# Token rows of attention move from the maxima's PSUM ring to the scores' ring, with a copy on ScalarE and the division on GpSimd

## What is computed

```python
xn = _layernorm(x, axis=-1)
x = x + _L0_attn_ref(xn, Wq, Wk, Wv) + _L0_ffn_ref(xn, w_gate, w_in, w_out)
```

## Time and profile before

| | |
|---|---|
| runs shown | 1012.16, 1012.63, 1015.68 us; median 1012.63 |
| the profiled execution | 1011.26 us, its span (first to last instruction) 1009.1 us |
| granted TensorE clock, mean of the span | 0.995 of full |
| busy share of the span | PE 98%, PEld 51%, DVE 79%, ACT 68%, POOL 17% |
| TensorE in the chain that ended last | 95% |
| attention loop, 380 to 980 us, in each 100 us | DVE 93 to 97 us, ACT 87 us, POOL 7 to 8 us |

### The profile page before, as it was taken

One profiled execution on the slowest core, in us unless ns is written; L12 is line 12 of the kernel. 1 busy time (PEld: TensorE's weight loads), 2 busy tenths in 40 slices (PEclk: granted clock), 3 DMA queues, 4 the chain that ended last, 5 costly groups with the idle time before them and its releaser, 6 DMA issues.

```text
span 1009.1 us, 20754 instructions
## 1 busy us (share of the span) xinstructions
PE 984.5 (98%) x7816; PEld 515.8 (51%) x7816; DVE 800.7 (79%) x1023; ACT 682.0 (68%) x1355; POOL 175.7 (17%) x325
## 2 busy tenths in 40 slices
PE   7999999999998999999999999999999999999995
PEld 6888888888876333333333333333333333333332
DVE  4343455543466899999999999999999999999967
ACT  2212333333322788888888888888888888888884
POOL 2001445444455100000000000000000000000000
PEclk9999999999999999999999999999999999999997
DMA  9967442223300233333333333333334333332204
GB/s 354 369 238 219 138 146 69 74 70 106 101 9 1 59 91 92 94 85 96 89 96 91 91 94 86 100 87 96 89 92 94 86 96 89 97 90 70 73 18 167
DMA packets 127043, 108.59 MB, mean 108 GB/s; under 512 B 81120, under 2 KB 102368, under 8 KB 126944
## 3 DMA queue, kind: packets, MB, share of 16 engines
q1 hardware_dynamic: 122720, 102.81, 35.3%
q10 hardware_dynamic: 4224, 4.46, 1.3%
HBM read 80.75 MB, written 42.21 MB: 122 GB/s over the span
## 4 chain that ended last, share of the span: by engine, by line
PE 95%; DVE 2%; issue 1%; DMA 1%; POOL 1%; SPq 0%; ACT 0%; POOLq 0%; DVEq 0%; ACTq 0%
PE ps L1034 28%; PE ps L1014 23%; PE ps L967 18%; PE ps L999 12%; PE ps L920 5%; PE ps L892 4%; PE ps L908 2%; PE ps L1045 1%; PE ps L1057 1%; DMA wp<-w_out_t 1%; PE ps L881 1%; DVE xn L851 0%; DVE stage L856 0%; DVE stage L870 0%; SPq L292 0%
## 5 line engine op out<-in xcount | busy, mean ns | idle before, releaser
L710 DVE TENSOR_REDUCE negm<-ps 128x1 f32<-128x1024 f32 x512 | 615.1, 1222 | 22.0 <-PE ps L999 14.7
L551 ACT ACTIVATE wp<-ps 128x512 f32<-128x512 f32 x680 | 369.6, 600 | 40.9 <-PE ps L1014 8.1
L1014 PE MATMUL ps<-qf,kf 50*128 50x512 f32 x1024 | 382.7, 449 | 0.0
L999 PE MATMUL ps<-kf,qf 48*128 48x512 f32 x1024 | 360.9, 445 | 0.9 <-DVE negm L710 0.9
L1014 PEld LDWEIGHTS ps<-qf,kf 50*128 50x128 f32 x1024 | 156.8, 185 | 201.9 <-ACT wp L551 107.0
L1034 PE MATMUL ps<-wp,vb 128*17 128x256 f32 x2720 | 212.6, 385 | 0.3 <-issue 0.2
L999 PEld LDWEIGHTS ps<-kf,qf 48*128 48x128 f32 x1024 | 144.1, 185 | 4.3 <-issue 3.9
L551 ACT ACTIVATE picks<-ps 128x512 f32<-128x512 f32 x172 | 103.3, 600 | 21.0 <-PE ps L1014 4.7
L701 DVE SCALAR_TENSOR_TENSOR acc<-ps,gates,acc 128x256 f32<-128x256 f32 x64 | 30.8, 482 | 99.1 <-PE ps L967 95.1
L1034 PEld LDWEIGHTS ps<-wp,vb 128*17 128x17 f32 x2720 | 46.0, 95 | 120.7 <-ACT vstage L551 49.6
L551 ACT ACTIVATE vstage<-ps 128x512 f32<-128x512 f32 x172 | 103.2, 600 | 1.1 <-PE ps L1014 1.1
(11 more groups left out here) (117 smaller groups left out, 821.1 us busy)
## 6 DMA issues: line engine op xcount, KB each, us to landing
qk_d<-stage SPq DMA_DIRECT2D x64, 256.0 KB
feat_d<-qk_d SPq DMA_DIRECT2D x64, 256.0 KB, 3.3
qf<-feat_d SPq DMA_DIRECT2D x128, 128.0 KB
qf<-feat_d SPq DMA_DIRECT2D x128, 64.0 KB
kf<-feat_d SPq DMA_DIRECT2D x128, 64.0 KB
v_d<-vstage ACTq DMA_DIRECT2D x8, 544.0 KB, 5.1
vb<-v_d SPq DMA_DIRECT2D x128, 34.0 KB, 2.4
acc<-x SPq DMA_DIRECT2D x8, 512.0 KB, 7.2
```

Source lines behind the costliest of these rows:

```text
L551: nc.scalar.activation(weight_tile(n, j, b)[:, h * HALF:(h + 1) * HALF], ps[:, ST_BANK[(2 * unit + b) % 3], :], ACT.Exp).then_inc(exp_done, 1)
L710: nc.vector.tensor_reduce(negm[:, n % 2, qt:qt + 1], ps[:, b:b + 2, :].rearrange("p b c -> p (b c)"), AX.X, ALU.max, negate=True).then_inc ...
L999: last = nc.tensor.matmul(ps[:, MAX_BANK[turn % 2] + half, :], qf[rows, u, qt * P:(qt + 1) * P], kf[rows, u, :], start=True, stop=True)
L1014: nc.tensor.matmul(ps[:, ST_BANK[(2 * unit + half) % 3], :], kf[rows, u, j * P:(j + 1) * P], qf[rows, u, h * HALF:(h + 1) * HALF], start=T ...
```

## The change

The token rows of a pair no longer have a turn among the maxima; they have one in the ring of the three scores' banks, behind the second score of unit 3 in odd heads. ScalarE copies them (`copy_rows`, 272 elements a partition) to `rows` in SBUF, behind `pv_out`. `pv_out` itself stands one exponential later, behind the second one of unit 3. GpSimd then raises the 16 sums to the power -1, multiplies, and adds to the tokens. Pair 31, the last, keeps VectorE's reciprocal and multiply. Two waits on `const_step` count one more memset, of the constant -1. The diff, without declarations of semaphores:

```diff
+        rows = choice[:, 0:16 * VW].rearrange("p (g c v) -> p g c v", g=4, c=4)
+        minus = sb("minus", [P, 4, 4])
...
-        for n in range(NB):
+        for n in range(NB - 2):
             for qt in range(NKT):
-                if n + 2 < NB:
-                    max_turn[n + 2, qt] = next_turn()
+                max_turn[n + 2, qt] = next_turn()
                 if n == 0 and qt == 2:
                     first_turn[1] = next_turn()
-                if qt == 2 * LAG - 1 and n % 2 == 1 and n > 1:
-                    row_turn[(n - 3) // 2] = next_turn()
-        row_turn[NB // 2 - 1] = next_turn()
+        last_turn = next_turn()
+
+        score_turn, row_turn, turn_user = {}, {}, []
+        for n in range(NB):
+            for unit in range(NKT * n, NKT * (n + 1)):
+                for half in range(2):
+                    score_turn[unit, half] = len(turn_user)
+                    turn_user.append(("exp", 2 * unit + half))
+                if unit == NKT * n + 2 * LAG - 1 and n % 2 == 1 and n > 1:
+                    row_turn[(n - 3) // 2] = len(turn_user)
+                    turn_user.append(("rows", (n - 3) // 2))
...
             def residual(pair):
-                pool.wait_ge(turn_done, row_turn[pair] + 1)
-                nc.gpsimd.tensor_tensor(xn[:, bass.ds(pair, 1), :].rearrange("p o d -> p (o d)"),
-                                        xn[:, bass.ds(pair, 1), :].rearrange("p o d -> p (o d)"),
-                                        att, ALU.add).then_inc(y_done, 1)
+                tile = xn[:, bass.ds(pair, 1), :].rearrange("p o d -> p (o d)")
+                if pair == NB // 2 - 1:
+                    pool.wait_ge(turn_done, last_turn + 1)
+                    nc.gpsimd.tensor_tensor(tile, tile, att, ALU.add).then_inc(y_done, 1)
+                    return
+                pool.wait_ge(rows_copied, pair + 1)
+                nc.gpsimd.tensor_tensor(rden[:], rows[:, :, :, DH], minus[:], ALU.pow).then_inc(rows_step, 1)
+                pool.wait_ge(rows_step, 2 * pair + 1)
+                nc.gpsimd.tensor_tensor(rows[:, :, :, 0:DH], rows[:, :, :, 0:DH],
+                                        rden[:].unsqueeze(3).to_broadcast([P, 4, 4, DH]), ALU.mult).then_inc(rows_step, 1)
+                pool.wait_ge(rows_step, 2 * pair + 2)
+                tile = xn[:, bass.ds(pair, 1), :].rearrange("p o (c g d) -> p (o g) c d", c=4, g=4)
+                nc.gpsimd.tensor_tensor(tile, tile, rows[:, :, :, 0:DH], ALU.add).then_inc(y_done, 1)
...
                 if n >= HELD:
-                    act.wait_ge(turn_ready, row_turn[(n - HELD) // 2] + 1)
+                    act.wait_ge(rows_ready, (n - HELD) // 2 + 1)
...
+            def copy_rows(pair):
+                act.wait_ge(rows_ready, pair + 1)
+                if pair:
+                    act.wait_ge(y_done, pair)
+                nc.scalar.copy(rows, ps[:, score_bank(row_turn[pair]), :].rearrange("p (g c v) -> p g c v", g=4, c=4)[:, :, :, 0:VW]
+                               ).then_inc(rows_copied, 1)
...
-                        if (j, h, b) == (LAG - 1, 1, 0) and n:
+                        if (j, h, b) == (LAG - 1, 1, 1) and n:
                             pv_out(n - 1)
+                    if j == LAG - 1 and n % 2 == 1 and n > 1:
+                        copy_rows((n - 3) // 2)
...
                     if n % 2 == 1 and n > 1:
-                        if qt == 2 * LAG - 1:
-                            normalise((n - 3) // 2)
-                        elif qt == NKT - 1:
+                        if qt == NKT - 1:
                             statistics((n - 3) // 2)
...
             for c in range(EARLY * NC // BATCH):
-                if c == BATCH - 1:
-                    normalise(NB // 2 - 2)
-                elif c == BATCH:
+                if c == BATCH:
                     statistics(NB // 2 - 2)
...
+            def free_score_bank(turn):
+                if turn >= len(ST_BANK):
+                    user, count = turn_user[turn - len(ST_BANK)]
+                    if user == "exp":
+                        pe.wait_ge(exp_done, count + 1)
+                    else:
+                        pe.wait_ge(rows_copied, count + 1)
...
-                if unit:
-                    pe.wait_ge(exp_done, 2 * unit - 2 + half)
+                free_score_bank(score_turn[unit, half])
...
             def to_token_rows(pair):
-                turn = row_turn[pair]
                 pe.wait_ge(pv_evac, 2 * pair + 2)
-                free_turn(turn)
+                last_pair = pair == NB // 2 - 1
+                if last_pair:
+                    bank = MAX_BANK[last_turn % 2]
+                    free_turn(last_turn)
+                else:
+                    bank = score_bank(row_turn[pair])
+                    free_score_bank(row_turn[pair])
```

More of the change, by code:

```diff
@@ L192, in attention_and_experts @@
         rden_done = sem("rden_done")
+        rows_ready = sem("rows_ready")
+        rows_copied = sem("rows_copied")
+        rows_step = sem("rows_step")
         y_done = sem("y_done")
@@ L202, in attention_and_experts @@
         o_out = sem("o_out", 4)
-        max_turn, row_turn, first_turn = {}, {}, {}
+        max_turn, first_turn = {}, {}
         def next_turn():
-            return len(max_turn) + len(row_turn) + len(first_turn)
+            return len(max_turn) + len(first_turn)
         for n in range(2):
@@ L213, in attention_and_experts, with score_bank @@
                     first_turn[0] = next_turn()
-        for n in range(NB):
+        for n in range(NB - 2):
             for qt in range(NKT):
-                if n + 2 < NB:
-                    max_turn[n + 2, qt] = next_turn()
+                max_turn[n + 2, qt] = next_turn()
                 if n == 0 and qt == 2:
                     first_turn[1] = next_turn()
-                if qt == 2 * LAG - 1 and n % 2 == 1 and n > 1:
-                    row_turn[(n - 3) // 2] = next_turn()
-        row_turn[NB // 2 - 1] = next_turn()
+        last_turn = next_turn()
[8 more added lines that the diff above has]
+                    turn_user.append(("rows", (n - 3) // 2))
+        def score_bank(turn):
+            return ST_BANK[turn % len(ST_BANK)]
         def sums_of(t):
@@ L363, in _ @@
             nc.gpsimd.memset(ident[:], 0.0).then_inc(const_step, 1)
-            for value, tile in ((-0.5, mhalf), (EPS, epst), (0.0, zero)):
+            for value, tile in ((-0.5, mhalf), (EPS, epst), (0.0, zero), (-1.0, minus)):
                 nc.gpsimd.memset(tile[:], value).then_inc(const_step, 1)
@@ L367, in _ @@
                 nc.gpsimd.memset(rank[:, e:e + 1], float(E - e)).then_inc(const_step, 1)
-            pool.wait_ge(const_step, 4 + E)
+            pool.wait_ge(const_step, 5 + E)
             nc.gpsimd.affine_select(out=ident[:], in_=ident[:], compare_op=ALU.not_equal, fill=1.0,
@@ L550, in exps @@
                     act.wait_ge(pv_done, used + 1)
-                nc.scalar.activation(weight_tile(n, j, b)[:, h * HALF:(h + 1) * HALF], ps[:, ST_BANK[(2 * unit + b) % 3], :],
+                nc.scalar.activation(weight_tile(n, j, b)[:, h * HALF:(h + 1) * HALF], ps[:, score_bank(score_turn[unit, b]), :],
                                      ACT.Exp).then_inc(exp_done, 1)
@@ L719, in normalise @@
             def normalise(pair):
-                turn = row_turn[pair]
-                o = ps[:, MAX_BANK[turn % 2], :].rearrange("p (g c v) -> p g c v", g=4, c=4)
-                dve.wait_ge(turn_ready, turn + 1)
+                o = ps[:, MAX_BANK[last_turn % 2], :].rearrange("p (g c v) -> p g c v", g=4, c=4)
+                dve.wait_ge(turn_ready, last_turn + 1)
+                dve.wait_ge(y_done, pair)
                 nc.vector.reciprocal(rden[:], o[:, :, :, DH]).then_inc(rden_done, 1)
-                dve.wait_ge(rden_done, pair + 1)
-                if pair:
-                    dve.wait_ge(y_done, pair)
+                dve.wait_ge(rden_done, 1)
                 nc.vector.tensor_tensor(att.rearrange("p (c g d) -> p g c d", c=4, g=4), o[:, :, :, 0:DH],
@@ L757, in _ @@
                 qk_lo_half(1, o)
-            dve.wait_ge(const_step, 5 + E)
+            dve.wait_ge(const_step, 6 + E)
             first_choice(0)
@@ L929, in _ @@
                 expert_product(0, s)
-            pe.wait_ge(const_step, 5 + E)
+            pe.wait_ge(const_step, 6 + E)
             transposes(0)
@@ L1013, in scores @@
                 rows = half_rows(half, SR)
-                nc.tensor.matmul(ps[:, ST_BANK[(2 * unit + half) % 3], :], kf[rows, u, j * P:(j + 1) * P],
+                nc.tensor.matmul(ps[:, score_bank(score_turn[unit, half]), :], kf[rows, u, j * P:(j + 1) * P],
                                  qf[rows, u, h * HALF:(h + 1) * HALF], start=True, stop=True
@@ L1040, in to_token_rows @@
             def to_token_rows(pair):
-                turn = row_turn[pair]
                 pe.wait_ge(pv_evac, 2 * pair + 2)
-                free_turn(turn)
```

(6 more changed lines are left out.)

## The result

The changed kernel takes **1004.12 us** in the median of 4 runs (1001.95 to 1004.91), against 1013.67 us of before (4 runs, one more than those shown above). The ratio is 0.9901, with a 95% interval from 0.9875 to 0.9927. The forecast was 1004.1 us, in a range from 999.5 to 1013.0. Two more comparisons, each on one chip, gave 0.9922 (0.9909 to 0.9934) and 0.9915 (0.9900 to 0.9930), so the gain is 8 to 10 us. The profiled execution took 1004.91 us.

A forecast was written before the change was run, and what follows sets the result against it. TensorE was taken as the bound, busy nearly all the time with 95% of the chain. The terms -5.1 - 4.3 + 0.9 = -8.5 us took the median from 1012.63 to 1004.1 us, range 999.5 to 1013.

The forecast's parts named there:

- The two stalls: TensorE waits in unit 4 of odd heads (1.39 us) and unit 5 of even heads (1.36), against 1.22 ordinarily.
- Row turn out of the maxima's ring: Unit 4 of odd heads needs an earlier reduce and falls to 1.22 us: 0.17 saved in 30 heads, 5.1 us.
- Copy one exponential later: Unit 5 of even heads falls from 1.36 to 1.22 us, L563 not later: 0.14 in 31 heads, 4.3 us.
- The sum for the heads: Savings in the attention heads, 5.1 and 4.3 us, from the row turn and the later copy.
- ScalarE's copy at 0.39, hidden: ScalarE's new copy of 272 elements takes 0.39 us, ends before unit 4's exponential is due, and costs nothing.
- The scores' ring, 0.: Row turn in the scores' ring of three: all waits hidden, 0 taken, at worst 0.1 in 30 units, 3 us.
- VectorE's relief, nothing by itself: VectorE loses reciprocal and multiply, 0.65 us a pair; it was not the bound, so nothing gained by itself.
- GpSimd's chain, 2.84 + 0.73 + 0.73: Power, multiply and add on GpSimd end 0.5 us before VectorE's statistics in odd heads, so hidden.
- The price of being late: At VectorE's statistics, chain time above 4.5 us, less 0.5 and 0.2 free, is paid 30 times.
- The rival: GpSimd's chain is late at odd heads' statistics: gain cancelled from 1.0 us too long, over 0.5% slower from 1.1; chance 0.18.
- The end, +0.9: In the last head VectorE's statistics wait about 1.5 us for GpSimd's chain: 0.9 us later, bounds 0 and 1.9.

The follow-up runs named there:

- the four copies of the experiment: Changed kernel with three more copies of 80 elements on ScalarE ahead of the copy of the rows: 1004.28 us, 0.9919 of before.

## Why the prediction was right

The two stalls were read rightly from the rows, and removing them gave what was named. The conditions under which they can be removed were not all named.

*Row turn out of the maxima's ring, 0.17 in 30 heads.* Right: 1.40 became 1.23. The kernel with only the copy moved keeps 1.41 there, and the one with VectorE dividing has 1.23, so it is the ring that did it. That it comes through as time has two conditions, below, which the prediction did not name.

*Copy one exponential later, 0.14 in 31 heads.* Right: 1.365 became 1.214, and the copy alone gave 4.5 us where 4.3 were named. L587 was not later, and unit 4's 1.29 stayed.

*The sum for the heads.* 9.4 us were named. From the first score of head 2 to that of head 62 the kernel before needs 623.4 us, the changed one 614.0 in the first profile and 615.3 in the second, so 8.1 to 9.3 less. Of the 1.3 us between these two profiles, 0.8 are in single units, most of them such as wait for the DMA of the maxima's rows (below).

*ScalarE's copy at 0.39, hidden.* 0.387 us, and the four copies of the experiment were hidden too. *The scores' ring, 0.* Right with the copy moved, and 15 us wrong without it; the prediction had the two edits as separate terms and did not say that the first needs the second.

*VectorE's relief, nothing by itself.* This step does not hold as it stands. It rested on VectorE not being the bound, by busy time. With the division on VectorE behind the reduce of unit 4, two waits of TensorE of 0.13 and 0.06 us come up in a pair, because the maxima may run only two reduces ahead, and they cost as much as the ring gives. Before, the division of 0.65 us filled the 0.65 us for which VectorE otherwise waits for the maxima of unit 4, which TensorE issues behind the transposes of the rows. In the changed kernel that room is from 614.30 to 614.95 us, and the copy of the rows is done only at 614.67; that place was not tried. The sum came out right all the same, since the relief was part of the change and its absence had been priced nowhere.

*GpSimd's chain, 2.84 + 0.73 + 0.73.* Measured 2.91 + 0.62 + 0.69, so the line through the two power times held to 16 elements, and multiply and add over runs of 16 elements cost no more than 256 in a row. The Trainium skill (GPSIMD Engine Reference, Performance pitfalls for Q7 kernels) warns of about 102 cycles for each small read command. These rows show no such cost for each run of 16. 0.65 us were to spare where 0.5 were named. The price of being late was named too low: not 0.2 us but less than 0.1 are free, and with 2.3 us of lateness TensorE's clock about doubles the price. The rival was real: 1.08 us more in the chain already make the kernel 0.4% slower than before; the forecast cancelled the gain at 1.0 and lost 0.5% at 1.1.

*The end, +0.9.* The step was right and short by 0.3: VectorE waited 2.28 us where about 1.5 were named. The power, beside VectorE's work in SBUF, took 3.31 and not 2.84, which is 0.5 of it.

The time of 1004.1 came from 9.4 and 0.9; measured were 8.1 to 9.3 for the heads and 1.2 for the end. That it was met to the tenth of a microsecond is luck: these terms are off by up to 1.3 and 0.3, and the kernel before itself has medians from 1012.4 to 1013.7.

## What to carry to other kernels

When the bound engine shows few waits, list its instructions from start to start by their place in the loop, and compare each with the ordinary one: here two places of 0.14 and 0.17 us, in a loop of 20.8, were the whole gain. In a ring of buffers the question is whose turn is two or three back, and a user that moves to another ring takes its wait along unless what it then waits for also moves; test the parts alone and together. Here the turn in the other ring gave 5 us with both other edits, cost 10 without the moved copy (unit 4 of 1.73 us in place of 1.40), and gave nothing with the division still on VectorE at the place tried. Work given to an idle engine has a deadline, the next instruction of another engine that stands in its queue; measure the room to it, since beyond it nearly all of the lateness is paid.

## What had not been expected of the hardware

- A wait of about 2 us of TensorE, once in each pair of heads, was followed within a few microseconds by 3.4 to 17.1 us at half its clock, in 29 of 30 pairs (not in the first), and this about doubled what the waits cost (147 us for a chain 3 us longer). In the profile in which TensorE waited 0.37 us a pair the clock did not fall once in the heads.
- The power on GpSimd takes 0.56, 0.86, 1.01 and 2.91 us for 1, 3, 4 and 16 elements a partition, about 0.15 us for each.
- TensorE's weight loads wait for the DMA that brings the maxima's rows 5 times in the profile of before and 15, 14 and 7 times in three profiles of the changed kernel. Most of these are the usual 0.42 us ahead of a weight load and cost nothing. What goes beyond, up to 0.4 us at a time, adds up to 0.1 us in before and to 0.4, 1.0 and 0.4 us in the changed kernel. That its shorter head is the reason is not shown: the kernel with only the copy moved has a longer head and 18 such waits.

```profile
PEld ps L1014 <- DMA qf<-ot: 2.2, 5, 0.5
```

```profile
PEld ps L1048 <- DMA qf<-ot: 6.7, 15, 0.8
```

These lines of the waits (engine, line, waited for; us in total, times, longest us), of before and of the changed kernel, count the usual 0.42 us ahead of a weight load in each.
